# A GRU over 1024 steps and a mixture of eight experts: from every expert for every token to sorted blocks of the chosen two, most of them between the recurrent matmuls

## What is computed

```python
def cell(h, x):
    gi = x @ W_ih + b_ih
    gh = h @ W_hh + b_hh
    r = sigmoid(i_r + h_r); z = sigmoid(i_z + h_z)
    n = tanh(i_n + r * h_n)
    return (1.0 - z) * n + z * h
...
logits = h / norm(h) @ router_w
rw, selected = top_k(softmax(logits), 2); rw = rw / sum(rw)
combine = sum(one_hot(selected) * rw)
for e in range(8):
    out = out + combine[:, e, None] * (h @ Wa[e] @ Wb[e])
return x + out
```

## Time and profile before

| | us |
|---|---|
| median of 3 runs | 10521.09 |
| lowest and highest of them | 10520.68, 10523.95 |
| the profiled execution's own time | 10528.88 |
| its span, from the first to the last instruction | 10527.1 |

### The profile page before, as it was taken

How to read it: one execution, slowest core, us unless ns; L and a number is a source line. 1 busy time by engine, 2 the same in 40 slices (tenths; PEclk the granted TensorE clock), 3 DMA queues, 4 the chain that set the end, 5 groups by cost and what they waited for, 6 DMA issues and landing times. The chain is left out here.

```text
span 10527.1 us, 516114 instructions
## 1 busy us (share of the span) xinstructions
PE 10330.0 (98%) x224296; PEld 5969.7 (57%) x224320; DVE 5471.8 (52%) x29233; ACT 1279.3 (12%) x4704; POOL 44.3 (0%) x63
## 2 busy tenths in 40 slices
PE   7999999999999999999999999999999999988999
PEld 4555555555555555555555555555555555554444
DVE  4555555555555555555555555555555555553111
ACT  2111111111111111111111111111111111001110
POOL 0000000000000000000000000000000000000000
PEclk9999999999999999999999999999999999999999
DMA  6111111111111111111111111111111111002111
GB/s 143 38 39 41 36 42 37 40 39 40 40 39 39 37 42 38 41 39 39 39 40 39 37 41 37 40 41 39 39 40 37 38 42 37 16 10 82 48 51 45
DMA packets 997464, 443.60 MB, mean 42 GB/s; under 512 B 507680, under 2 KB 978720, under 8 KB 994080
## 3 DMA queue, kind: packets, MB, share of 16 engines
q1 hardware_dynamic: 992352, 397.12, 14.9%
q0 software_dynamic: 2752, 12.61, 0.4%
HBM read 325.66 MB, written 83.89 MB: 39 GB/s over the span
## 5 line engine op out<-in xcount | busy, mean ns | idle before, releaser
L437 PE MATMUL gh_ps<-w_hh_parts,h_parts 128*12 128x288 bf16 (+1 forms) x196608 | 8368.4, 327 | 121.2 <-DVE h_parts L362 61.0
L437 PEld LDWEIGHTS gh_ps<-w_hh_parts,h_parts 128*12 128x12 bf16 x196608 | 4804.5, 88 | 3392.5 <-DVE h_parts L362 380.8
L311 DVE STREAM_TRANSPOSE gh<-gh_ps 128x288 f32<-128x288 f32 (+1 forms) x2048 | 1192.5, 582 | 2530.5 <-PE gh_ps L437 2530.5
L456 PE MATMUL gi_ps<-x_t,w_ih_tile 128*32 128x256 f32 x24576 | 1658.3, 381 | 49.6 <-DMA w_ih_tile<-in_L_cond_W_ih 49.6
L408 ACT ACTIVATE gate<-pre 128x24 f32<-128x24 f32 (+1 forms) x2048 | 470.4, 230 | 7205.4 <-DVE pre L324 7205.4
L456 PEld LDWEIGHTS gi_ps<-x_t,w_ih_tile 128*32 128x32 f32 x24576 | 741.5, 111 | 637.9 <-DMA w_ih_tile<-in_L_cond_W_ih 56.3
L317 DVE TENSOR_REDUCE gh_sum<-gh 128x36 f32<-128x108 f32 (+1 forms) x2048 | 651.9, 318 | 71.0
L332 DVE TENSOR_TENSOR r_cand<-h_cand,gate 128x12 f32<-128x12 f32 (+1 forms) x2048 | 360.3, 176 | 610.5 <-ACT gate L408 610.5
L344 DVE TENSOR_TENSOR zn<-one_minus_z,cand 128x12 f32<-128x12 f32 (+1 forms) x2048 | 360.3, 176 | 428.7 <-ACT cand L411 427.8
L411 ACT ACTIVATE cand<-cand_in 128x12 f32<-128x12 f32 (+1 forms) x2048 | 441.7, 216 | 1112.9 <-DVE cand_in L335 1112.9
L759 PE MATMUL ps_u<-ht,wa 128*128 128x512 f32 x1024 | 449.4, 593 | 0.4
(11 more groups left out here) (75 smaller groups left out, 1189.7 us busy)
## 6 DMA issues: line engine op xcount, KB each, us to landing
w_ih_tile<-in_L_cond_W_ih SPq DMA_DIRECT2D x1548, 128.0 KB, 2.7
gi_scratch<-gi_stage SPq DMA_DIRECT2D x384, 128.0 KB, 1.9
gi<-gi_scratch SPq DMA_DIRECT2D x128, 384.0 KB, 4.6
x_raw<-in_x SPq DMA_DIRECT2D x272, 64.0 KB, 2.0
h_scratch<-h SPq DMA_DIRECT2D x512, 32.0 KB, 1.5
h_raw<-h_scratch SPq DMA_DIRECT2D x8, 2048.0 KB, 7.3
x_nat<-in_x SPq DMA_DIRECT2D x8, 2048.0 KB, 11.7
out<-y_out SPq DMA_DIRECT2D x64, 256.0 KB, 2.0
```

The source lines that it names most:

```text
L311: nc.vector.transpose(gh[k][:, :, :, :], ps[k][sp_][:, 0:GATES * n * Q].rearrange("p (q c i) -> p q c i", q=GATES, i=Q))\
L437: ins = nc.tensor.matmul(ps[k_out][t % 2][j * Q:j * Q + SPLIT * B, 0:GATES * (o1 - o0) * Q], h_parts[:, (t - 1) % 2, c, :, :].rearrange("p ...
L456: ins = nc.tensor.matmul(ps_i[m % 2][j * Q:(j + 1) * Q, 0:COLS], w_i[m % WR][:, c, j * Q:(j + 1) * Q], x_t[:, c, :, :].rearrange("p t b -> ...
```

## The change

**Routing in windows.** The state now goes into a ring of 64 steps (`ring`). Every 32 steps are a window v (4 sequences x 32 steps = 128 tokens): VectorE transposes it to one token per partition (`turn_window`, at steps 1 and 33, after both parts), SyncE stores that to `h_scratch` in four transfers, TensorE makes the logits from the ring (`logits`, steps 3 and 35), GpSimd squares and sums (`window`) and, by linked instructions, finds the two chosen experts, TensorE counts how many tokens before each lane chose each expert (`places`, steps 11 and 43), and GpSimd writes for each token and choice a record (token, weight, row of the state) into the list of its expert, by an indirect transfer. Whenever a list reaches a multiple of 128 records a block is entered into a table of 64 (`where`).

**Blocks in the recurrence.** From the fourth of the 16 blocks of steps on (`FIRST` = 3), four blocks of 128 records are computed in each (`PER` = 4), at the steps in `TILE_H`, `TILE_U` and `TILE_Y`: 52 in all. GpSimd gathers the block's list, its rows of the state, Wa and Wb of its expert; VectorE transposes the rows (`turn_rows`), TensorE makes `hidden` (32 matmuls of 32 x 128) and in two later steps `output` (4 matmuls of 32 x 512 each), ScalarE copies and scales, and GpSimd adds the rows to `out` in memory with an accumulating indirect transfer (`finish`). `out` is first filled with x, by SyncE, block of steps by block of steps (`copy_x`). Wa is first copied in two layouts, in 8 and 64 transfers.

**The rest.** `routed_ffn` goes. `leftover` does 12 more entries of the table and the 8 unfilled lists, 20 blocks of at most 128 records, in a program block of its own: gathers on GpSimd, transposes on TensorE by an identity, both products, and gather, add and scatter of the output rows in two halves.

**Storage.** The W_hh staging tiles become the ring and the expert's weights (`shared`), x_raw also holds gathered rows, w_ih has two slots in the loop instead of three (`WL`), x is loaded at step 59 instead of 2, and the start state is laid out after the conversion of W_hh and the first projection. The last block of steps is written out, not looped.

The core of the diff (lines of the new kernel; comments and the empty lines left out):

```diff
+REC = 4
+FAR = 1 << 20
+WIN = 32
+FIRST = 3
+PER = 4
+TILE_HN = {1: 0, 33: 1}
+TILE_LOGITS = {3: 0, 35: 1}
+TILE_SUMSQ = {6: 0, 38: 1}
+TILE_PLACE = {11: 0, 43: 1}
+TILE_H = {18: 0, 23: 1, 50: 2, 55: 3}
+TILE_U = {19: 0, 26: 1, 51: 2, 58: 3}
+TILE_Y = {22: (0, 0), 23: (0, 1), 29: (1, 0), 30: (1, 1), 54: (2, 0), 55: (2, 1), 62: (3, 0), 63: (3, 1)}
+X_LOAD = 59
...
+            def store_h(v):
+                sp.wait_ge(hn_ready, v + 1)
+                for j in range(NQ):
+                    sp.dma_start(hist[bass.ds(v * P, P), j, :].rearrange("(b t) f -> t b f", t=WIN),
+                                 hn[j * Q:(j + 1) * Q, :, :]).then_inc(hist_out, DMA)
+            def copy_x(n):
+                sp.dma_start(out[:, bass.ds(n * TB, TB), :].rearrange("b t d -> t b d"),
+                             x[:, bass.ds(n * TB, TB), :].rearrange("b t d -> t b d")).then_inc(x_copied, DMA)
...
+            for e in range(E):
+                sp.dma_start(wa_dram[e * P:(e + 1) * P, :].rearrange("p (c r) -> p c r", r=P),
+                             w_a[e, :, :].rearrange("(c p) r -> p c r", p=P)).then_inc(wa_out, DMA)
+            for e in range(E):
+                for a in range(NQ):
+                    mine = slice(e * P + a * Q, e * P + (a + 1) * Q)
+                    for hf in range(2):
+                        sp.dma_start(
+                            route["wa_rows"][mine, :].rearrange("i (j h r) -> h i j r", j=NQ, h=2)[hf, :, :, :],
+                            w_a[e, :, :].rearrange("(h a j i) r -> a h i j r", a=NQ, h=2, i=Q)[a, hf, :, :, :])\
+                          .then_inc(wa_rows_out, DMA)
+            def steps(n, experts, last):
+                for t in range(TB):
+                    if t in TILE_HN:
+                        store_h(n * 2 + TILE_HN[t])
+                    if t == 4:
+                        copy_x(n)
+                    if not last and t == X_LOAD:
+                        if experts:
+                            sp.wait_ge(u_done, n * PER + (START + PER - FIRST * PER))
+                        else:
+                            sp.wait_ge(xt_ready, (n + 2) * NC)
+                        load_x((n + 2) % NB)
...
+            def fold(o, a):
+                n = a.shape[2]
+                while n > 2:
+                    n //= 2
+                    tt(a[:, :, 0:n], a[:, :, 0:n], a[:, :, n:2 * n], ALU.add)
+                tt(o, a[:, :, 0], a[:, :, 1], ALU.add)
+            def window(v):
+                pool.wait_ge(hn_ready, v + 1)
+                if v:
+                    squares = expert.rearrange("p (b f) -> p b f", b=B)
+                    tt(squares, hn, hn, ALU.mult)
+                    pool.sem_inc(hn_read, 1)
+                    fold(sumsq[:, :], squares)
...
+                pool.sem_inc(ss_ready, 1)
+                pool.wait_ge(lg_ready, START + v + 1)
+                if v:
+                    ts(norm[:, :], lg[:, E:E + 1], 1e-24, None, ALU.max, ALU.bypass)
+                    tt(rnorm[:, :], norm[:, :], root[:, :], ALU.pow)
+                    tt(logit[:, :], lg[:, 0:E], rnorm[:, :].broadcast_to([P, E]), ALU.mult)
...
+                pool.sem_inc(taken_ready, 1)
+                pool.wait_ge(place_ready, 2 * (START + v + 1))
+                if not v:
+                    return
+                tt(pos[:, :], place[:, 0:E], count[:, :], ALU.add)
...
+                spread = expert[:, 0:FULL * E].rearrange("p (k e) -> p k e", e=E)
+                tt(spread, over(block_id[:, :], E), along(kid[:, :], FULL), ALU.subtract)
+                ts(spread, spread, 0.0, None, ALU.is_equal, ALU.bypass)
+                tt(spread, spread, along(value[:, :], FULL), ALU.mult)
+                fold(block_sum, spread)
...
+            def fetch_rows(k, v):
+                if k:
+                    pool.wait_ge(ht_ready, k)
+                for g in range(NQ):
+                    nc.gpsimd.indirect_dma_start(
+                        out=raw[:, g, :], out_offset=None, in_=hist_rows[0:v * P * NQ, :],
+                        in_offset=bass.IndirectOffsetOnAxis(ap=idx_h[:, g:g + 1], axis=0)).then_inc(raw_in, DMA)
+            def fetch_wa(k):
+                nc.gpsimd.indirect_dma_start(
+                    out=expert, out_offset=None, in_=wa_dram,
+                    in_offset=bass.IndirectOffsetOnAxis(ap=idx_w[k % 2][:, :], axis=0)).then_inc(expert_in, DMA)
+                if k:
+                    pool.wait_ge(y_out, DMA * k)
+                    pool.sem_inc(y_free, 1)
+            def fetch_wb(k):
+                pool.wait_ge(u_done, START + k + 1)
+                nc.gpsimd.indirect_dma_start(
+                    out=expert, out_offset=None, in_=wb_rows,
+                    in_offset=bass.IndirectOffsetOnAxis(ap=idx_w[k % 2][:, :], axis=0)).then_inc(expert_in, DMA)
+            def finish(k, n):
+                pool.wait_ge(y_ready, START + 2 * (k + 1))
+                pool.wait_ge(x_copied, DMA * n)
+                nc.gpsimd.indirect_dma_start(
+                    out=out_rows, out_offset=bass.IndirectOffsetOnAxis(ap=list_n[k % 2][:, 0:1].bitcast(U32), axis=0),
+                    in_=yrow, in_offset=None, compute_op=ALU.add).then_inc(y_out, DMA)
+            for n in range(NB):
+                k = blocks_before(n)
+                if k > 0:
+                    finish(k - 1, n)
+                window(2 * n)
+                if k == 0:
+                    pool.wait_ge(wa_out, DMA * E)
+                if k >= 0:
+                    pool.wait_ge(xt_ready, NC * min(n + 2, NB))
+                    pool.wait_ge(hist_out, DMA * NQ * (START + 2 * n + 1))
+                    fetch_lists(k)
+                    fetch_rows(k, 2 * n + 1)
+                    fetch_wa(k)
+                    fetch_wb(k)
+                    fetch_lists(k + 1)
+                    fetch_rows(k + 1, 2 * n + 1)
+                    finish(k, n + 1)
+                    fetch_wa(k + 1)
+                    fetch_wb(k + 1)
+                    finish(k + 1, n + 1)
+                window(2 * n + 1)
...
+                if k == 0 and t % WIN == 0:
+                    dve.wait_ge(lg_done, blk * 2 + (START + t // WIN))
...
+            def turn_window(blk, half):
+                dve.wait_ge(hn_read, blk * 2 + (START + half))
+                dve.wait_ge(hist_out, (blk * 2 + (START + half)) * (DMA * NQ))
+                w0 = WIN * (1 - half)
+                nc.vector.transpose(hn.rearrange("p b (c i) -> p b c i", i=Q),
+                                    ring[:, w0:w0 + WIN, :, :].rearrange("p t c b -> p b c t")).then_inc(hn_ready, 1)
+            def turn_rows(k):
+                dve.wait_ge(raw_in, (k + 1) * (DMA * NQ))
+                dve.wait_ge(u_done, k + START)
+                nc.vector.transpose(ht.rearrange("p c (g i) -> p g c i", i=Q),
+                                    raw.rearrange("p g (c i) -> p g c i", i=Q)).then_inc(ht_ready, 1)
...
+            def logits(v, half):
+                pe.wait_ge(lg_ready, v + START)
+                w0 = WIN * (1 - half)
+                for c in range(NC):
+                    for b in range(B):
+                        ins = nc.tensor.matmul(ps_r[b * Q:(b + 1) * Q, 0:E], ring[:, w0:w0 + WIN, c, b], rw[:, c, :],
+                                               start=(c == 0), stop=(c == NC - 1))
+                ins.then_inc(lg_done, 1)
...
+            def places(v):
+                pe.wait_ge(taken_ready, v + 1)
+                pe.wait_ge(place_ready, (v + START) * 2)
+                for j in range(NQ):
+                    nc.tensor.matmul(ps_r[j * Q:(j + 1) * Q, 2 * E:3 * E], before[:, j * Q:(j + 1) * Q], taken[:, :],
+                                     start=True, stop=True)
+                for j in range(NQ):
+                    ins = nc.tensor.matmul(ps_r[j * Q:(j + 1) * Q, 3 * E:4 * E], every[:, :], taken[:, :],
+                                           start=True, stop=True)
+                ins.then_inc(place_done, 1)
+            def hidden(k):
+                pe.wait_ge(ht_ready, k + 1)
+                pe.wait_ge(expert_in, (k * 2 + 1) * DMA)
+                pe.wait_ge(us_ready, k + START)
+                for c in range(NC):
+                    for j in range(NQ):
+                        ins = nc.tensor.matmul(ps_r[j * Q:(j + 1) * Q, P:2 * P],
+                                               expert[:, c * P + j * Q:c * P + (j + 1) * Q], ht[:, c, :],
+                                               start=(c == 0), stop=(c == NC - 1))
+                ins.then_inc(u_done, 1)
+            def output(k, hf):
+                if hf == 0:
+                    pe.wait_ge(us_ready, k + (START + 1))
+                    pe.wait_ge(expert_in, (k * 2 + 2) * DMA)
+                pe.wait_ge(y_ready, k * 2 + (START + hf))
+                for j in range(NQ):
+                    ins = nc.tensor.matmul(ps_y[j * Q:(j + 1) * Q, 0:HALF], us[:, j * Q:(j + 1) * Q],
```

(65 more changed lines are left out.)

967 lines of the change are left out of this document (571 added, 396 removed).

## The result

| | before | after |
|---|---|---|
| time, median of 5 runs | 10521.56 us | 10570.32 us (10565.49 to 10573.15) |
| profiled execution, span | 10528.9, 10527.1 us | 10565.49, 10563.7 us |
| last 288-column transpose of the recurrence starts | 9573.9 us | 10095.7 us |
| from there to the end of the span | 953.2 us | 468.0 us |
| 64 steps, mean of the twelve blocks 3 to 14 | 588.4 us | 630.2 us |

The ratio is 1.0045 [1.0034, 1.0056]: slower by 0.45%, where 10270 us was forecast. The expert stage did go. The recurrence grew by 522 us (407 forecast). Closing window and tail take 462 us, from VectorE's last recurrent instruction at 10101.9 (289 forecast); the 468 of the table begin some 6 us earlier.

The account below looks back on a forecast made before the run. TensorE, busy 98%, was taken as the bound, with 0.1 to 0.2 us slack per VectorE chain. Terms 202 + 83 + 107 + 15 + 46 + 243 - 946.6 = -250.6 gave 10270 us against the median, range 10090 to 10560.

Parts of the forecast that it names:

- experts between steps: 52 expert blocks in the recurrence: TensorE's `hidden` 2.16 us and `output` 1.72 us each lengthen the steps, +202 us.
- routing on TensorE: 32 windows in the recurrence: 64 added weight loads each, plus small ones for squares and places, 2.6 us a window, +83 us.
- GpSimd beside VectorE: Recurrence: GpSimd's large window instructions, 4.8 us a window, stop VectorE while it is inside a chain, +107 us.
- start: Kernel start: start state laid out later, and copies of Wa delay a w_ih column; +15 us.
- closing window: Routing of the last window after the last step, with nothing to hide it: +46 us, ends 30 and 70.
- tail: Last 20 expert blocks, bound by GpSimd's issue of indirect transfers plus landing: +243 us, ends 170 and 420.
- the rival of dear transfers: Indirect transfers at 1.9 us each and 4.6 us landing lengthen the tail by 173 us, hidden in the recurrence: 10443 us, chance 0.18.
- I am wrong if a wait of TensorE on a transfer appears within the blocks: Sign against the forecast: TensorE or VectorE waiting on a transfer within the recurrence's blocks; no size given.
- removed stage: Old expert stage, from VectorE's last recurrent instruction at 9580.47 to the span's end, goes: -946.6 us.
- no cost of VectorE's transposes of x and of the window: VectorE's six transposes of 1024 elements per 64 steps, 2.05 us each, fit its 2.52 us idle time: 0.
- fixed slots that never miss their data: Opposite of the rival that engines wait for GpSimd at steps written into the code: 260 us, 10530 us, chance 0.08.
- The port rival: Recurrence: GpSimd's instructions hold the shared port whole against VectorE's chains, 431 us, 10594 us, slower; chance 0.12.

Follow-up runs that it names:

- t1_tail: Changed kernel with the tail's GpSimd queue reordered (rows gathered one block earlier, gathers from out before those of the weights): 10130.8 us.
- w1: Changed kernel without the 52 expert blocks between the steps (lists, gathers, matmuls, accumulating writes); windows and tail stay: 10162.4 us.
- c1: Changed kernel with t1_tail's tail order and the window's squares and sums made by ScalarE instead of GpSimd: 10072.3 us.
- t2: The same program as t1_tail, measured again in another set, beside the unaltered changed kernel: 10417.6 us.

## Why the prediction was wrong

"Faster" was wrong; the time was 300 us too low, and 10570 lies just outside the range. Term by term, the steps read where gaps are absent (t1_tail), so that the gaps stand by themselves (the recurrence's terms sum to 521 us, 522 were measured):

| term | forecast | measured | from |
|---|---|---|---|
| experts between steps | 202 | 168 | 12.9 us per 64 steps x 13: t1_tail's 19.8 less w1's 8.9 without its list writes (2.0) |
| routing on TensorE | 83 | 42 | 32 x 1.3, steps 3 and 35 |
| GpSimd beside VectorE | 107 | 59 | 10130.8 - 10072.3 (t1 and c1) |
| start | 15 | 14 | 4.2 to the first transpose, 10 of block 0's 15.6 (its steps 0 and 4) |
| **gaps of TensorE beside gathers** | **none** | **287** | 13 x (630.2 - 608.2), and t2 against t1 |
| last block | 0 | about -48 | below |
| closing window | 46 | 40 | 10101.9 to 10141.5 |
| **tail** | **243** | **422** | 10141.5 to 10563.7 |

*The failed step is that SyncE's and GpSimd's transfers were priced only by whoever waits for their data.* The part on the experts said that all they cost is TensorE's own 3.88 us, and the rival of dear transfers that in the recurrence their cost stays hidden. What the runs showed in its place: bursts of indirect gathers make TensorE stand, 287 us in all. "I am wrong if a wait of TensorE on a transfer appears within the blocks" was the nearest to it; what appeared is a wait that names no transfer.

*The last block* was put at nothing without a reason, though the change writes it out where before has a loop of eight turns of 8 steps. In before's last block every eighth step takes 14 us instead of 8.7, seven times. TensorE stands there for "issue", here after steps 31 and 55:

```profile
9278.55 1.14 PE L437 MATMUL gh_ps<-w_hh_parts,h_parts 128*12 128x288 bf16 x29 [2.07 <-issue]
9280.23 0.41 SPq L222 DMA_DIRECT2D gi<-gi_scratch  x1
9281.50 8.77 PE L437 MATMUL gh_ps<-w_hh_parts,h_parts 128*12 128x288 bf16 x163 [1.81 <-issue]
9504.09 1.14 PE L437 MATMUL gh_ps<-w_hh_parts,h_parts 128*12 128x288 bf16 x29 [2.14 <-issue]
```

The load of gi (L222) is not the cause: the first wait is over before it is issued, and after step 55 there is none, yet TensorE stands again in two waits. The places are the turns of the loop. In each of the 14 waits a packet of q8 lands, and TensorE resumes some 1.5 us later; so here late instructions are the likely meaning. The turn of the loop over blocks shows the same in before: step 63 takes 11.9 us, and 3.2 less in the last turn. After, with its last block written out and the same 128 loads of gi, has none of the seven. That is 37 us, and steps of 8.52 for 8.70 us are 11 more; together they are the 48 by which its last block is shorter than the terms make it. No run has the loop alone changed.

*The tail* failed in the step "GpSimd is [the bound]". I summed what GpSimd issues and added one landing, 11.9 us a block, but did not walk the queue in order. One turn holds GpSimd's wait for outputs, behind a TensorE stage that waits for the rows asked for just before: 25.8 us. With the order mended the sum nearly comes out: 13.6 us a block in t1_tail. 0.957 us per indirect transfer and its landing were right, so the rival of dear transfers fell.

*Right:* removed stage, no cost of VectorE's transposes of x and of the window, start, closing window, fixed slots that never miss their data. *Right in kind, off in size:* `hidden` costs a step 1.75 us, for 2.16. Logits cost 1.3 for 1.95. The port rival had the mechanism: whole instructions are waited for. But it is decided by the few that are large; the three VectorE instructions that large ones held up cost 1.85 us a window, where 4.8 x 0.72 = 3.5 was forecast and 11.5 would have made the kernel slower. By the figure of the Trainium skill, "GPSIMD Engine Reference", section 3.1 (4497 ns for 2048 elements), the term would have been some 220 us, an estimate that is further off. In this trace 1024 elements take 1.89 us, where half of that figure is 2.25.

In sets without gaps the unaltered kernel would take 10130.8 + 153 = 10284 us (an estimate; it was not run there), near the forecast, but by errors that cancel: 168 us too much in the recurrence (407 for 239) and 173 too little behind it (289 for 462). That nearness would have been luck.

## What to carry to other kernels

Where TensorE runs a long unrolled body, ask of every transfer not only who waits for its data but also what TensorE does beside it. In the trace of before, look where it already waits for "issue", and hold these places against the program: here they were the turns of a loop, and with the loop of the last block 37 us went. Spread indirect gathers over the steps instead of issuing them back to back: 225 us here, for a wait and two moved slots. In a chain of stages walk one turn of the slowest queue instruction by instruction, since a wait ahead of work that is ready doubled the tail; and give a half-idle engine the large elementwise work that another shares a port with.

## What the runs showed of the hardware that was not expected

- Indirect transfers of 128 rows, four or five in 6 us, made TensorE stand 3 to 5 us with its data ready. Plain transfers of the same bytes on the same queue did not (630 and 612 us per 64 steps), and scattered or consecutive rows made no difference (630.2, 629.7). One gather of rows per 9 us step cost it 0.1 us at most. What it stands for is open: hardly an instruction packet lands in these pauses (16 of 242).
- These gaps showed in four sets of measurements and not in two, for one and the same program (10417.6 and 10130.8 us), while the kernel before stayed within 3 us.
- At a turn of its loop TensorE stood too, some 3 us after 64 steps and some 5 us after 8; in each of the 14 waits of the last block an instruction packet landed (before).
- Two VectorE instructions of 0.17 us with two SBUF operands ended within 0.04 us of the end of a GpSimd instruction of 1.9 and 1.3 us that had begun before them, and one with a single tensor operand within 0.03 us of the end of one of 0.7; a transpose from PSUM beside it took its usual 0.48 us.
- ScalarE's four squares with sums of 256 elements per window, in place of GpSimd's, cost the steps nothing.
